# Summing squares by a transpose and a VectorE reduction in place of a product with ones

## What is computed

```
h = relu(hypergraph_conv(x, adj, W1, b1))      # 128 nodes x 512
h = layer_norm(h, gamma, beta)                 # needs mean and variance over the 512
y = hypergraph_conv(h, adj, W2, b2)            # 128 nodes x 256
x = layer_norm(x + (y + x))
```

## Time and profile before

| what | value |
|---|---|
| median of 3 runs | 1393.01 us (1392.85 to 1393.94) |
| profiled execution, its own time | 1393.31 us |
| its span, first to last instruction | 1391.2 us |
| mean granted TensorE clock, share of full | 0.997 |
| TensorE (PE) busy | 1376.9 us, 99% of the span |
| its weight loads (PEld) | 1335.9 us, 96% |
| VectorE (DVE) busy | 1134.6 us, 82% |
| ScalarE (ACT) busy | 1122.7 us, 81% |
| GpSimd (POOL) busy | 1003.6 us, 72% |

### The profile page before, as it was taken

One profiled execution on the slowest core, in us unless ns is written; L12 is line 12 of the kernel. 1 busy time (PEld: TensorE's weight loads), 2 busy tenths in 40 slices (PEclk: granted clock), 3 DMA queues, 4 the chain that ended last, 5 costly groups with the idle time before them and its releaser, 6 DMA issues.

```text
span 1391.2 us, 35333 instructions
## 1 busy us (share of the span) xinstructions
PE 1376.9 (99%) x10946; PEld 1335.9 (96%) x10946; DVE 1134.6 (82%) x4092; ACT 1122.7 (81%) x2639; POOL 1003.6 (72%) x1059
## 2 busy tenths in 40 slices
PE   8999999999999999999999999999999999999997
PEld 8999999999999999999999999999999999999996
DVE  7888788888887887788888878878888888888896
ACT  6777887887888878878878888888788788887776
POOL 5758778778778787787787787777877877877531
PEclk9999999999999999999999999999999999999999
DMA  4100110110100101101101101011011011010000
GB/s 143 36 20 20 40 39 20 39 40 20 39 29 31 39 21 39 39 20 40 39 20 40 32 28 39 21 39 39 21 39 39 20 40 37 23 40 21 8 22 34
DMA packets 29961, 47.17 MB, mean 34 GB/s; under 512 B 3408, under 2 KB 12240, under 8 KB 29776
## 3 DMA queue, kind: packets, MB, share of 16 engines
q1 hardware_dynamic: 29776, 44.91, 10.1%
HBM read 28.12 MB, written 16.78 MB: 32 GB/s over the span
## 4 chain that ended last, share of the span: by engine, by line
PE 98%; ACT 1%; issue 0%; DVE 0%; DMA 0%; SPq 0%; ACTq 0%; DVEq 0%
PE psum L374 95%; PE psum L473 2%; PE psum L417 1%; DMA n_s<-w2T_in 0%; ACT x L1010 0%; ACT tk L1172 0%; ACT h_hi L991 0%; DVE w2c_lo L1785 0%; DVE w2g L1767 0%; ACT w2c_hi L991 0%; ACT r_f L1015 0%; SPq L291 0%; ACT h_f L1015 0%; DVE n_st L1575 0%; DVE n_s L260 0%
## 5 line engine op out<-in xcount | busy, mean ns | idle before, releaser
L208 POOL TENSOR_TENSOR h_lo<-h_f,h_hi 128x512 fp32r<-128x512 f32 x120 | 154.9, 1291 | 93.6 <-ACT h_hi L991 93.4
L1010 ACT ACTIVATE x<-n_s,n_shift,n_rstd 128x256 f32<-128x256 f32 x384 | 208.0, 590 | 4.2 <-DVE n_shift L1599 4.1
L215 POOL TENSOR_TENSOR r_lo<-r_f,r_hi 128x512 fp32r<-128x512 f32 x123 | 158.7, 1292 | 44.1 <-ACT r_hi L991 43.9
L2229 POOL TENSOR_TENSOR n_s<-tk,mask 128x512 f32<-128x512 f32 x60 | 62.5, 1041 | 154.1 <-DVE mask L1652 133.0
L1575 DVE BATCH_NORM_STATS2 n_st<-n_s 128x6 f32<-128x256 f32 x384 | 141.9, 412 | 2.2
L374 PE MATMUL psum<-v_hi,h_hi 128*128 128x256 f32 x512 | 137.8, 292 | 2.0 <-ACT h_hi L991 2.0
L374 PE MATMUL psum<-A_f,x 128*128 128x128 f32 x1024 | 135.5, 275 | 0.6 <-ACT x L1010 0.5
L1015 ACT ACTIVATE h_f<-psum,columns 128x256 f32<-128x256 f32 x256 | 107.6, 472 | 34.8 <-PE psum L374 34.7
L374 PE MATMUL psum<-v_lo,h_hi 128*128 128x256 f32 x512 | 133.3, 282 | 0.0
L374 PE MATMUL psum<-gx_hi,w1T_hi 128*128 128x256 f32 x512 | 132.3, 281 | 0.0
L374 PE MATMUL psum<-gx_hi,w1T_lo 128*128 128x256 f32 x512 | 131.9, 281 | 0.0
(11 more groups left out here) (173 smaller groups left out, 5200.1 us busy)
## 6 DMA issues: line engine op xcount, KB each, us to landing
x_in<-x_in_dram SPq DMA_DIRECT2D x64, 256.0 KB, 2.8
out<-x SPq DMA_DIRECT2D x64, 256.0 KB, 2.0
at_in<-adjT SPq DMA_DIRECT2D x64, 128.0 KB, 2.2
x<-v_in SPq DMA_DIRECT2D x3, 256.0 KB, 5.7
n_s<-w2T_in SPq DMA_DIRECT2D x2, 256.0 KB, 3.3
r_f<-w1T_in SPq DMA_DIRECT2D x2, 256.0 KB, 5.1
h_f<-wab_in SPq DMA_DIRECT2D x2, 256.0 KB, 5.6
rows<-rows_in SPq DMA_DIRECT2D x1, 256.0 KB, 6.0
```

Source lines behind the costliest of these rows:

```text
L208: return e.tensor_tensor(dst[1][:], src, f(dst[0][:]), ALU.subtract).then_inc(signal, 1)
L215: e.tensor_tensor(r_s[1][:, half], r_f[:, half], f(r_s[0][:, half]), ALU.subtract).then_inc(r_lo[h], 1)
L1010: last = act.activation(dst[:, g, :], nm.s[:, g, :], ACT.Identity, scale=nm.rstd[:, g:g + 1], bias=nm.shift[:, g:g + 1])
L2229: pool.tensor_tensor(n4.s[:], tk[:], bc(mask[:], [C, 2, D], 2), ALU.mult).then_inc(tk_masked, 1)
```

## The change

For pairs 0 to 60 (all but the last three), `squares` no longer multiplies `sq1` by ones. TensorE transposes the two 128 x 128 tiles of `sq1` into columns 384 to 511 of P's two banks, which puts the nodes in the partitions. VectorE then sums along the 128 columns with one TENSOR_REDUCE over both graphs, into a new tile `h_sq` in SBUF (`add_columns`), ahead of the two instructions of `wide_var`, the first of which now reads `h_sq`. The reduction waits for `pe_did["P"]` and for ACT's `square_mean`. Nothing in the order of any engine's list is moved. Several one-purpose semaphores are merged into counting ones (`dn_step`, `deg_step`, `w2_step`), with the same waits at the same places.

```diff
             def squares(p):
                 pe.wait_ge(sq_sum, upto(p))
+                if p + 1 < LAST:
+                    if p == 0:
+                        pe.wait_ge(eye_loaded, 16)
+                    for g in range(2):
+                        last = pe.transpose(psum[:, bank("P", p) + g, 3 * C:4 * C], sq1[:, g, :], ident[:])
+                    last.then_inc(pe_did["P"], 1)
+                    return
                 for g in range(2):
                     last = mm(psum[:, bank("P", p) + g, D + 2:D + 3], sq1[:, g, :], ones[:, 0:1], True, True)
                 last.then_inc(pe_did["P"], 1)
...
+            def add_columns(p):
+                b = bank("P", p)
+                dve.wait_ge(pe_did["P"], upto(p))
+                dve.wait_ge(hm2, upto(p))
+                if begun(p - 1):
+                    dve.wait_ge(hv, upto(p - 1))
+                dve.tensor_reduce(h_sq[:], psum[:, b:b + 2, 3 * C:4 * C], AX_X, ALU.add).then_inc(sq_added, 1)
+
             def wide_var(p):
                 b = bank("P", p)
+                if p + 1 < LAST:
+                    add_columns(p)
+                    dve.wait_ge(sq_added, upto(p))
                 h_var = psum[:, b:b + 2, D + 4]
                 dve.wait_ge(hm2, upto(p))
-                dve.scalar_tensor_tensor(out=h_var, in0=psum[:, b:b + 2, D + 2], scalar=1.0 / DH,
+                dve.scalar_tensor_tensor(out=h_var, in0=h_sq[:] if p + 1 < LAST else psum[:, b:b + 2, D + 2],
+                                         scalar=1.0 / DH,
                                          in1=h_mean2[:], op0=ALU.mult, op1=ALU.subtract).then_inc(hv, 1)
...
-                dve.tensor_reduce(dn, psum[:, both, 2 * C:2 * C + 2], AX_X, ALU.add).then_inc(dn_0, 1)
-                dve.wait_ge(dn_0, upto(p))
-                dve.tensor_scalar(dn_max[:], dn, TINY, None, ALU.max).then_inc(dn_1, 1)
-                dve.wait_ge(dn_1, upto(p))
+                dve.tensor_reduce(dn, psum[:, both, 2 * C:2 * C + 2], AX_X, ALU.add).then_inc(dn_step, 1)
+                dve.wait_ge(dn_step, 3 * p + 1)
+                dve.tensor_scalar(dn_max[:], dn, TINY, None, ALU.max).then_inc(dn_step, 1)
+                dve.wait_ge(dn_step, 3 * p + 2)
```

More of the change, by code:

```diff
@@ L95, in build @@
         sq, sq2, sq1 = sb("sq", [KH, 2, C]), sb("sq2", [2, 2, C]), sb("sq1", [2, C])
-        h_mean2 = sb("h_mean2", [2])
+        h_mean2, h_sq = sb("h_mean2", [2]), sb("h_sq", [2])
         h_veps, h_std, h_rstd = sb("h_veps", [2]), sb("h_std", [2]), sb("h_rstd", [2])
@@ L150, in build @@
         table_loaded = sem("table_loaded")
-        consts_step, beta_made, w1_hi, w1_lo, w2_scaled, w2_mean, w2_centred, w2c_hi, w2c_lo = (
-            sem(s) for s in ("consts_step", "beta_made", "w1_hi", "w1_lo", "w2_scaled", "w2_mean",
-                             "w2_centred", "w2c_hi", "w2c_lo"))
+        consts_step, beta_made, w1_hi, w1_lo, w2_scaled, w2_step = (
+            sem(s) for s in ("consts_step", "beta_made", "w1_hi", "w1_lo", "w2_scaled", "w2_step"))
         betaW_made, wab_hi, wab_lo, v_hi, v_lo, b2_made = (
@@ L160, in build @@
             sem(s) for s in ("ht_made", "ht_counted", "be_max", "be_made", "be_hi", "be_lo", "bh_high", "bh_made"))
-        dn_0, dn_1, dn_2, dn_3, gl_made, gd_made = (sem(s) for s in ("dn_0", "dn_1", "dn_2", "dn_3", "gl_made", "gd_made"))
+        dn_step, dinv_made, gl_made, gd_made = (sem(s) for s in ("dn_step", "dinv_made", "gl_made", "gd_made"))
         w_hi, w_lo, gt_made, gx_hi, gx_lo = (sem(s) for s in ("w_hi", "w_lo", "gt_made", "gx_hi", "gx_lo"))
@@ L165, in build @@
         sq_made, sq_half, sq_sum = sem("sq_made"), sem("sq_half"), sem("sq_sum")
+        sq_added = sem("sq_added")
         hm2, hv, hve, hstd, hrstd = (sem(s) for s in ("h_mean2", "h_var", "h_veps", "h_std", "h_rstd"))
-        deg_max, deg_inv = sem("deg_max"), sem("deg_inv")
+        deg_step = sem("deg_step")
         p_made, p_hi, p_lo, xb_made = sem("p_made"), sem("p_hi"), sem("p_lo"), sem("xb_made")
@@ L440, in P @@
                 if p == 0 and h == 0:
-                    pe.wait_ge(w2c_lo, 1)
+                    pe.wait_ge(w2_step, 4)
                 outs = [(psum[:, bank("P", p) + g, 0:D + 2],
@@ L607, in fill @@
                 pe.wait_ge(gt_hi, 1)
-                pe.wait_ge(w2_mean, 1)
+                pe.wait_ge(w2_step, 1)
                 G(2)
@@ L1202, in round_w2 @@
             def round_w2():
-                act.wait_ge(w2_centred, 1)
-                copy(w2c_s[0][:, :, 0:D], w2g[:]).then_inc(w2c_hi, 1)
+                act.wait_ge(w2_step, 2)
+                copy(w2c_s[0][:, :, 0:D], w2g[:]).then_inc(w2_step, 1)
             def fill():
@@ L1658, in scale_G @@
                 dve.wait_ge(pe_did["G"], upto(p))
-                dve.tensor_reduce(dn, psum[:, both, 2 * C:2 * C + 2], AX_X, ALU.add).then_inc(dn_0, 1)
-                dve.wait_ge(dn_0, upto(p))
-                dve.tensor_scalar(dn_max[:], dn, TINY, None, ALU.max).then_inc(dn_1, 1)
-                dve.wait_ge(dn_1, upto(p))
-                dve.reciprocal(dn_inv[:], dn_max[:]).then_inc(dn_2, 1)
-                dve.wait_ge(dn_2, upto(p))
+                dve.tensor_reduce(dn, psum[:, both, 2 * C:2 * C + 2], AX_X, ALU.add).then_inc(dn_step, 1)
+                dve.wait_ge(dn_step, 3 * p + 1)
+                dve.tensor_scalar(dn_max[:], dn, TINY, None, ALU.max).then_inc(dn_step, 1)
+                dve.wait_ge(dn_step, 3 * p + 2)
+                dve.reciprocal(dn_inv[:], dn_max[:]).then_inc(dn_step, 1)
+                dve.wait_ge(dn_step, 3 * p + 3)
                 dve.scalar_tensor_tensor(out=dinv[:], in0=dn, scalar=0.0, in1=dn_inv[:],
-                                         op0=ALU.is_gt, op1=ALU.mult).then_inc(dn_3, 1)
-                dve.wait_ge(dn_3, upto(p))
+                                         op0=ALU.is_gt, op1=ALU.mult).then_inc(dinv_made, 1)
+                dve.wait_ge(dinv_made, upto(p))
                 if begun(p - 1):
@@ L1724, in node_degree @@
                 dve.wait_ge(pe_did["AXB"], upto(p))
-                dve.tensor_scalar(degm[:], psum[:, b:b + 2, D], DEG_EPS, None, ALU.max).then_inc(deg_max, 1)
-                dve.wait_ge(deg_max, upto(p))
-                dve.reciprocal(rdeg[:], degm[:]).then_inc(deg_inv, 1)
+                dve.tensor_scalar(degm[:], psum[:, b:b + 2, D], DEG_EPS, None, ALU.max).then_inc(deg_step, 1)
+                dve.wait_ge(deg_step, 2 * p + 1)
+                dve.reciprocal(rdeg[:], degm[:]).then_inc(deg_step, 1)
             def make_agg(p):
@@ L1731, in make_agg @@
                 dve.wait_ge(xa_out, upto(p))
-                dve.wait_ge(deg_inv, upto(p))
+                dve.wait_ge(deg_step, 2 * p + 2)
                 for g in range(2):
@@ L1771, in mean_w2 @@
                 dve.wait_ge(pe_did["W2"], 1)
-                dve.tensor_scalar(w2mean[:], psum[:, bank("W2", 0), 0:D], 1.0 / DH, None, ALU.mult).then_inc(w2_mean, 1)
+                dve.tensor_scalar(w2mean[:], psum[:, bank("W2", 0), 0:D], 1.0 / DH, None, ALU.mult).then_inc(w2_step, 1)
             def centre_w2():
-                dve.wait_ge(w2_mean, 1)
+                dve.wait_ge(w2_step, 1)
                 dve.wait_ge(w2_scaled, KH)
-                dve.tensor_tensor(w2g[:], w2g[:], bc(w2mean[:], [C, KH, D], 1), ALU.subtract).then_inc(w2_centred, 1)
+                dve.tensor_tensor(w2g[:], w2g[:], bc(w2mean[:], [C, KH, D], 1), ALU.subtract).then_inc(w2_step, 1)
             def high_w2():
-                dve.wait_ge(w2_centred, 1)
-                dve.tensor_copy(w2c_s[0][:, :, 0:D], w2g[:]).then_inc(w2c_hi, 1)
+                dve.wait_ge(w2_step, 2)
+                dve.tensor_copy(w2c_s[0][:, :, 0:D], w2g[:]).then_inc(w2_step, 1)
             def low_w2():
-                dve.wait_ge(w2c_hi, 1)
+                dve.wait_ge(w2_step, 3)
                 dve.tensor_tensor(w2c_s[1][:, :, 0:D], w2g[:], f(w2c_s[0][:, :, 0:D]),
-                                  ALU.subtract).then_inc(w2c_lo, 1)
+                                  ALU.subtract).then_inc(w2_step, 1)
             def spread_beta():
```

## The result

The kernel after takes 1478.86 us (median of 4 runs, 1478.07 to 1481.26) against 1392.97 for the one before: a ratio of 1.0618, 95% interval 1.0599 to 1.0636. Slower was forecast, but by 25 us and not by 86, and the result lies outside the range.

The account below looks back on a forecast made before the run. TensorE's own train of passes was taken to bound the kernel. 55 iterations x 0.45 = 24.8 us, less 0.1 in the fill, gave a 1415.9 us span; plus 2.1, less 0.3, forecast 1417.7 us, range 1405 to 1428.

Parts of the forecast that it names:

- On VectorE: VectorE's variance chain: one added reduction of 0.42 us plus 0.04 us handing over makes the variance 0.46 us later.
- TensorE stands in front of Ax3 for x3: TensorE's load of x3, queued on ScalarE behind the root: a wait of about 0.65 us, some 55 times.
- the start stays where it is: Start of VectorE's chain: held by the shift of n4, not moved by faster TensorE, so the whole 0.46 us is delay.
- the whole delay on the iteration: Body iterations at Ax3: each gets longer by 0.46 less a 0.01 us margin, 0.45 us.
- The fill: First six pairs: savings and delays together about -0.1 us, with ends of -1.2 and +2.8.
- the saving on TensorE: TensorE's squares and Tr stages: four transposes in a row take 0.43 us instead of 0.63, saving 0.20 per pair.
- The saving is kept: Rival at Ax3: x3 has room, the reduction is hidden, TensorE saves 12.2 us, giving 1380.8 us; chance 0.12.
- The clock falls: Rival on TensorE: granted clock drops to 1.2 GHz for some part, giving about 1441 us; chance 0.04.
- TensorE's busy time did not fall by 12 us: Sign in the changed kernel's profile: PE's busy time should fall by about 12 us while the span grows by about 25.

Follow-up runs that it names:

- sums_in_psum: The kernel after, with the reduction writing its sums into PSUM, where the product with ones put them, instead of h_sq in SBUF: 1417.88 us, ratio 1.0172.
- dummy_reduction: The kernel before, products with ones kept, plus a 0.42 us VectorE reduction that nobody reads ahead of the variance: 1421.05 us (one run).
- x3_first: sums_in_psum with make_x3 moved ahead of root_h in ScalarE's list and copy_GT behind the root: 1389.68 us, ratio 0.9971.
- no_reduction: The kernel after without the reduction; the variance reads one transposed square from PSUM in place of the sum: 1387.47 us, ratio 0.9954.
- x3_first_body: x3_first with transposes and reduction only for the 55 body pairs; the first six pairs keep the product with ones: 1386.82 us, ratio 0.9948.
- x3_first_no_reduction: no_reduction with ScalarE's new order, make_x3 ahead of root_h and copy_GT behind it: 1384.5 us, ratio 0.9937.

## Why the prediction was wrong, and where it was right

**The step that failed** is in "On VectorE": it has the variance come 0.46 us later, the reduction and one handing over, and so prices wide_var's own two instructions as they were. The diff moves the first one's squares from PSUM to `h_sq` in SBUF. That instruction went from 0.17 to 1.29 us, because GpSimd's xb was under way by then in each of the 55 iterations. This is 1.12 of the 1.49 us per iteration, 62 us of the 86; sums_in_psum, which undoes nothing else, takes them back. GpSimd was passed over in the forecast because none of its steps was moved. What counted was what it was doing when VectorE reached for a second operand in SBUF.

By the Trainium skill (SBUF — State Buffer, Who interferes with whom), a VectorE instruction with two SBUF inputs and a GpSimd instruction that reads SBUF exclude each other: whichever starts first holds the shared port pair for its whole length. The trace agrees: the step ended 0.02 us after xb, and with xb in halves it took 0.72 us. That the resource is this port pair is the page's statement; the runs show that operand place and GpSimd's activity are both needed.

**Right, with its place.** TensorE stands in front of Ax3 for x3, which waits on ScalarE behind the root: 56 times, in the kernel after (91.5 us) and in sums_in_psum (31.0 us, 0.55 each and not 0.65). dummy_reduction shows that the delay alone does it, and x3_first that x3's place in ScalarE's list is the reason.

**Terms mis-sized.** That sums_in_psum came out at 1417.88 against a forecast of 1417.7 is partly luck, of errors that cancel. The iteration there is 21.59 us (1151.26 to 1172.85), 0.38 longer and not 0.45. The reduction starts 0.83 us after the squares' first load (717.59 to 718.42), where the variance started 0.86 after it before (705.14 - 704.28), so "the start stays where it is" was wrong by 0.03 us: the mean square had been holding it a little as well. And R makes up 0.08 us of the wait, as in no_reduction; the forecast put the whole delay on the iteration. The other way goes 0.04 us: from xT to the next squares an iteration takes 10.61 us there and 10.58 before (medians). The fill was put at -0.1 us and the drain at nothing; in sums_in_psum the epsilon step of pair 5 is 3.4 us late (114.11 against 110.74), the drain is 1.5 us longer (why stays open), and x3_first_body gains 2.9 us by leaving the fill alone. Last, the saving on TensorE was put at 0.20 us per pair. The two stages with the transposes do take 0.19 less, but the iteration without any wait for x3 (x3_first_no_reduction) is only 0.14 shorter; there too it is longer from xT to the next squares, by 0.03 us, and why stays open.

**The rivals.** "The saving is kept" did not hold in the kernel after, and to look at the most occupied engine alone was not enough: TensorE's saving by itself brought 6.5 us, and 8.8 once ScalarE's order was changed, but in the kernel after the delay of the variance took back more. "The clock falls" did not either: in the kernel after, with eight transposes and a stand of 1.65 us in each iteration, the granted clock over one iteration was still 1.00:

```profile
748.00:770.70 22.70, 21.25 (x170) 20.51 (x169) 18.84 (x66) 17.47 (x41) 16.25 (x19) 1.00 0.09 31
```

TensorE's busy time did not fall by 12 us as foretold; it rose by 2.6. In that window it is 21.25 us of 22.70, though TensorE stands for 1.65: the listed lengths of products run on into the stand. In x3_first_no_reduction, where there is no such stand, it is 1366.6 us, 10.3 below the kernel before. A busy total does not show a saving of passes where an engine stands often.

## What to carry to other kernels

When a change moves an operand from PSUM to SBUF, price the instructions that read it anew: look which of their tensors now lie in SBUF, and what GpSimd does at that moment. When an engine is 99% busy, look for the tile that reaches it just in time (here 0.06 us before it is loaded): the chain that makes this tile has no room, whatever the busy shares say. A delay in it is a wait of the full engine, and of the passes saved ahead of it a part is waited away there (0.10 of 0.19 us in no_reduction); how much of a wait is lost in the end shows in the length of the iteration, not in the wait. An instruction list that is kept in order can hold back a tile of another layer; moving that tile ahead cost nothing, and it took 28 us off the kernel with the reduction.

## What the runs showed of the hardware that was not expected

The order of start decides, and by very little. In the fill of the kernel after, pair 5's step started 0.02 us ahead of xb and took 0.17 us; pair 3's started while xb was under way and ended 0.03 us after it:

```profile
63.15 1.30 POOL L240 TENSOR_TENSOR xb<-x_in,b2half 128x512 f32<-128x512 f32 x1
63.34 1.14 DVE L1717 SCALAR_TENSOR_TENSOR psum<-h_sq,h_mean 128x2 f32<-128x2 f32 x1
...
114.62 0.17 DVE L1717 SCALAR_TENSOR_TENSOR psum<-h_sq,h_mean 128x2 f32<-128x2 f32 x1
114.64 1.31 POOL L240 TENSOR_TENSOR xb<-x_in,b2half 128x512 f32<-128x512 f32 x1
```

In all 55 iterations of the body GpSimd is ahead, by 0.03 to 0.04 us in 53 of them, so that a step of 128 x 2 elements pays nearly the whole length of a GpSimd instruction. In the two others it is ahead by 0.36 and 0.38 us, and the step is the shorter for it; it still ends 0.03 us after xb:

```profile
658.38 0.42 DVE L1708 TENSOR_REDUCE h_sq<-psum 128x2 f32<-128x256 f32 x1
658.48 1.30 POOL L240 TENSOR_TENSOR xb<-x_in,b2half 128x512 f32<-128x512 f32 x1
658.84 0.97 DVE L1717 SCALAR_TENSOR_TENSOR psum<-h_sq,h_mean 128x2 f32<-128x2 f32 x1
```

It need not be xb: in the fill, pair 1's step (35.70, 0.24 us) ends 0.03 us after another GpSimd instruction, the one that makes BH (35.30 + 0.61). The reduction, whose input lies in PSUM, is not held in the rows above: it takes its 0.42 us while xb starts. The profile lists the stand of the step as busy time of VectorE, not as a wait: only the duration, against the same instruction elsewhere, gives it away.
